# Second attention: turned probabilities applied as full fp32 on four 32-column tiles instead of as two fp32r parts on the whole array

## What is computed

```python
q = (x @ Wq).reshape(b, t, N_HEADS, HEAD_DIM).transpose(0, 2, 1, 3)
k, v = ...                       # N_KV = 8 heads, rotated q and k
k_h = jnp.repeat(k, GROUP_SIZE, axis=1)      # GROUP_SIZE = 4
v_h = jnp.repeat(v, GROUP_SIZE, axis=1)
scores = jnp.einsum('bhqd,bhkd->bhqk', q, k_h) / math.sqrt(HEAD_DIM)
scores = jnp.where(causal[None, None], jnp.finfo(scores.dtype).min, scores)
attn = jax.nn.softmax(scores, axis=-1)
ctx = jnp.einsum('bhqk,bhkd->bhqd', attn, v_h)
ctx = ctx.transpose(0, 2, 1, 3).reshape(b, t, D_OUT)
return ctx @ Wo
```

## Time and profile before

| | us |
|---|---|
| median of 3 runs | 1215.43 (1215.10 to 1216.92) |
| the profiled execution | 1214.89 |
| its span, first to last instruction | 1213.3 |
| in it: slots 4 to 62 of the loop, start to start | 198.24 |
| TensorE busy in these 198.24 | 196.56 |
| ScalarE busy in these | 197.38 |
| VectorE busy in these | 169.76 |
| GpSimd busy in these | 141.02 |

### The profile page before, as it was taken

How to read it: one execution, slowest core, us unless ns; L and a number is a source line. 1 busy time by engine, 2 the same in 40 slices (tenths; PEclk the granted TensorE clock), 3 DMA queues, 4 the chain that set the end, 5 groups by cost and what they waited for, 6 DMA issues and landing times. The chain is left out here.

```text
span 1213.3 us, 21135 instructions
## 1 busy us (share of the span) xinstructions
PE 1180.8 (97%) x6698; PEld 1023.2 (84%) x6698; DVE 799.6 (66%) x2575; ACT 752.5 (62%) x1758; POOL 548.3 (45%) x519
## 2 busy tenths in 40 slices
PE   7899999999999999999999999999999999999997
PEld 6788888888888888888888788888887999999886
DVE  6757776667766677766777722223458888888685
ACT  6656765566655567655665454441129999999624
POOL 4554454444533554534533233331136766676400
PEclk9999999999999999999999999999999999999999
DMA  6011110011110111101000022220002213220001
GB/s 223 18 44 36 35 36 28 22 43 27 46 34 12 44 36 35 36 27 35 27 1 27 18 70 78 61 97 1 18 20 53 65 41 108 48 48 21 1 1 70
DMA packets 30368, 51.28 MB, mean 42 GB/s; under 512 B 5680, under 2 KB 6576, under 8 KB 30256
## 3 DMA queue, kind: packets, MB, share of 16 engines
q1 hardware_dynamic: 29680, 48.85, 13.7%
q10 hardware_dynamic: 576, 1.05, 0.2%
HBM read 38.35 MB, written 2.10 MB: 33 GB/s over the span
## 5 line engine op out<-in xcount | busy, mean ns | idle before, releaser
L487 POOL TENSOR_TENSOR turned<-turned,sin 128x512 f32<-128x512 f32 x73 | 94.4, 1293 | 311.5 <-ACT turned L347 311.5
L363 ACT ACTIVATE probs<-probs,neg_max 128x256 f32<-128x256 f32 (+1 forms) x256 | 119.8, 473 | 14.0 <-DVE neg_max L580 14.0
L1484 ACT ACTIVATE a_probs<-a_probs,a_neg_max 128x512 f32<-128x512 f32 (+3 forms) x256 | 123.2, 571 | 0.1
L1720 DVE CUSTOM_DVE_ANT_0 a_probs<-bank,a_mask 128x512 f32<-128x512 f32 (+3 forms) x256 | 109.7, 485 | 0.2 <-PE bank L1949 0.2
L490 POOL TENSOR_TENSOR turned<-turned,by_cos 128x512 f32<-128x512 f32 x73 | 101.1, 1385 | 5.7
L96 PE MATMUL bank<-wo_hi,oT_hi 128*128 128x512 f32 x256 | 100.3, 392 | 1.7 <-DVE oT_lo L643 1.7
L734 PE MATMUL bank<-xT_hi,wq_hi 128*128 128x512 f32 x256 | 101.7, 397 | 0.0
L734 PE MATMUL bank<-xT_lo,wq_hi 128*128 128x512 f32 x256 | 100.2, 391 | 0.0
L734 PE MATMUL bank<-xT_hi,wq_lo 128*128 128x512 f32 x256 | 100.1, 391 | 0.0
L96 PE MATMUL bank<-wo_hi,oT_lo 128*128 128x512 f32 x256 | 99.9, 390 | 0.0
L96 PE MATMUL bank<-wo_lo,oT_hi 128*128 128x512 f32 x256 | 99.7, 389 | 0.0
(11 more groups left out here) (239 smaller groups left out, 3454.0 us busy)
## 6 DMA issues: line engine op xcount, KB each, us to landing
staged<-weights SPq DMA_DIRECT2D x70, 256.0 KB, 2.7
f_staged<-weights_f SPq DMA_DIRECT2D x33, 256.0 KB, 2.7
a_q_stack<-a_qT_hi SPq DMA_DIRECT2D x64, 64.0 KB, 2.0
rows<-x_rows SPq DMA_DIRECT2D x2, 1024.0 KB, 7.4
a_k_stack<-a_kT_hi SPq DMA_DIRECT2D x64, 32.0 KB, 2.0
a_q_stack<-a_qT_lo SPq DMA_DIRECT2D x32, 64.0 KB, 2.0
out<-rows SPq DMA_DIRECT2D x8, 256.0 KB, 2.0
a_raw<-weights_qkv SPq DMA_DIRECT2D x4, 384.0 KB, 4.9
```

What stands on the lines that cost most here:

```text
L363: act.activation(probs[:, s % 2, h, 0:width], probs[:, s % 2, h, 0:width], ACT.Exp, bias=neg_max[:, s % 2, h:h + 1], scale=SCALE0, accum_o ...
L487: pool.tensor_tensor(at, at, sin[:, :], ALU.mult).then_inc(sin_done, 1)
L1484: act.activation(row_probs(s, qt), row_probs(s, qt), ACT.Exp, bias=neg_max[:, h, qt:qt + 1], scale=-1.0).then_inc(exp_done, 1)
L1720: dve.tensor_tensor_reduce(row_probs(s, qt), ps_s[bank][:, at:at + seen], mask[:, SEQ - seen:SEQ], -SCALE1, HIGHEST, ALU.add, ALU.min, neg ...
```

## The change

A head's turned probabilities are no longer split. They are copied out of PSUM as plain fp32 into a ring of six heads, `pT`: piece 0 by VectorE, pieces 1 and 2 by ScalarE. GpSimd does nothing to them. The values stay plain fp32 too, in `v_tok`, 18 columns for a key tile (16 values, a one, and one more); a stationary operand is 32 columns of it, of which 17 count.

`apply` now works on a unit: for each key tile, four products, one for each head of the group, with the same 32 stationary columns, each to its own 32 partitions of one PSUM bank, on its own 32-column tile of the array (`tile_position`). The products are full fp32. Key tiles 0 and 3 come in the first slot after the unit, 1 and 2 in the second. Two banks take turns as `ps_o`. One result bank holds four heads instead of two, so `evacuate` (moved from ScalarE to VectorE), `turn_output` and `join` come once a unit instead of twice; `join` multiplies from PSUM straight to `o_tok`, and `finish` is gone.

The diff, cut to its core:

```diff
-HALF = P // 2
-ONE_AT = 2 * HD1
-PAIRS1 = 2 * UNITS1
+RING = 6
+VALUE_COLS = HD1 + 2
+HEAD_ROWS = P // GROUP1
+APPLY_KEYS = ((0, 3), (1, 2))
...
-            def high_turned(s):
-                if s >= 2:
-                    act.wait_ge(applied, s - 1)
-                act.wait_ge(pT_ready, PIECES * s + 1)
-                act.activation(pT_raw[:, s % 2, :], ps_t[0][:, :], ACT.Copy).then_inc(pT_copied, 1)
+            def copy_turned(s):
+                if s >= RING:
+                    act.wait_ge(applied, 2 * ((s - RING) // GROUP1 + 1))
                 for piece in (1, 2):
...
-                    act.activation(pT_hi[:, s % 2, piece, 0:width], ps_t[piece][:, 0:width], ACT.Copy).then_inc(pT_hi_done, 1)
-
-            def evacuate(n):
-                act.wait_ge(applied, 2 * (n + 1))
-                if n >= 1:
-                    act.wait_ge(o_turned, n)
-                act.activation(oT_now[:, :], ps_o[:, :], ACT.Copy).then_inc(o_read, 1)
+                    act.activation(pT[:, s % RING, at:at + width], ps_t[piece][:, 0:width], ACT.Copy).then_inc(pT_act, 1)
...
+            def copy_turned(s):
+                if s >= RING:
+                    dve.wait_ge(applied, 2 * ((s - RING) // GROUP1 + 1))
+                dve.wait_ge(pT_ready, PIECES * s + 1)
+                dve.tensor_copy(pT[:, s % RING, 0:SEQ], ps_t[0][:, :]).then_inc(pT_dve, 1)
+
+            def evacuate(n):
+                dve.wait_ge(applied, 2 * (n + 1))
+                if n >= 1:
+                    dve.wait_ge(o_turned, n)
+                dve.tensor_copy(oT_now[:, :], ps_o[n % 2][:, :]).then_inc(o_read, 1)
...
+                dve.reciprocal(inv_sum[:, :, :], turned[:, :, :, HD1]).then_inc(inv_done, 1)
                 dve.wait_ge(inv_done, n + 1)
-                dve.tensor_tensor(o_sum[:, :, :, :], turned[:, :, :, 0:HD1], o_sum[:, :, :, :], ALU.add).then_inc(summed, 1)
+                dve.tensor_tensor(o_tok[...].rearrange(
+                    "p t (h d) -> p t h d", d=HD1), turned[:, :, :, 0:HD1],
+                                  inv_sum[...].broadcast_to(
+                                      [P, SEQ_TILES, GROUP1, HD1]), ALU.mult).then_inc(finished, 1)
...
-            def apply(s):
+            def apply(u, part):
...
+                if u >= 2 and part == 0:
+                    pe.wait_ge(finished, u - 1)
+                if part == 0:
+                    pe.wait_ge(pT_dve, GROUP1 * (u + 1))
+                    pe.wait_ge(pT_act, 2 * GROUP1 * (u + 1))
+                for kb in APPLY_KEYS[part]:
                     piece, at = TURNED_AT[kb]
-                    width = SEQ - kb * P
-                    for part in (pT_hi, pT_lo):
-                        mm = pe.matmul(ps_o[:, kb * P:SEQ], v_now[:, u % 2, kb, window:window + P],
-                                       part[:, s % 2, piece, at:at + width],
-                                       start=(h % 2 == 0 and kb == 0 and part is pT_hi),
-                                       stop=(h % 2 == 1 and kb == KEY_TILES[-1] and part is pT_lo),
-                                       skip_group_check=True)
+                    at += piece * SEQ
+                    value = (u * SEQ_TILES + kb) * VALUE_COLS
+                    for h in range(GROUP1):
+                        mm = pe.matmul(ps_o[u % 2][h * HEAD_ROWS:(h + 1) * HEAD_ROWS, kb * P:SEQ],
+                                       v_flat[:, value:value + HEAD_ROWS],
+                                       pT[:, (GROUP1 * u + h) % RING, at:at + SEQ - kb * P],
+                                       start=(kb == APPLY_KEYS[0][0]), stop=(kb == APPLY_KEYS[-1][-1]),
+                                       skip_group_check=True, tile_position=(0, h * HEAD_ROWS))
                 mm.then_inc(applied, 1)
...
-            for s in range(SLOTS1 + 1):
+            for s in range(SLOTS1 + 2):
                 if s < SLOTS1:
                     turn(s)
-                if BEHIND_APPLY <= s < SLOTS1 + BEHIND_APPLY:
-                    apply(s - BEHIND_APPLY)
+                if s >= GROUP1 and s % GROUP1 < 2:
+                    apply(s // GROUP1 - 1, s % GROUP1)
...
-                if s % 2 == 1 and s >= 3:
-                    turn_output((s - 3) // 2)
+                if s % GROUP1 == 3 and s >= GROUP1:
+                    turn_output(s // GROUP1 - 1)
```

More of the change, by code:

```diff
@@ L1282, in attention1 @@
         k_tok = sb("k_tok", [P, TILES, KV1 * HD1])
-        v_tok = sb("v_tok", [P, UNITS1, SEQ_TILES, HD1])
+        v_flat = sb("v_tok", [P, UNITS1 * SEQ_TILES * VALUE_COLS + HEAD_ROWS])
+        v_tok = v_flat[:, 0:UNITS1 * SEQ_TILES * VALUE_COLS].rearrange("p (u t c) -> p u t c", u=UNITS1, t=SEQ_TILES)
         o_tok = q_tok
         probs = sb("probs", [P, GROUP1, HEAD_PROBS])
[L1289 to L1293, removed]
+        pT = over("pT", [P, RING, HEAD_PROBS], xT_at)
+        b_at = aligned(nc.sbuf_base)
+        sb("b_place", [P, 2, D])
         oT_now = sb("oT_now", [P, SEQ])
-        o_sum = sb("o_sum", [P, SEQ_TILES, 2, HD1])
         by_at = aligned(nc.sbuf_base)
@@ L1451, in _ @@
                     sp.dma_start(small[:, :], small_in).then_inc(main_in, 16)
-                    for n in range(2):
-                        sp.dma_start(main_raw[n][:, :, :], w_f1[2 * n:2 * n + 2].rearrange("k p c -> p k c")[:, :, 0:D]).then_inc(main_in, 16)
+                    for place, some in ((main_first, slice(0, 1)), (main_rest, slice(1, KC))):
+                        sp.dma_start(place[:, :, :], w_f1[some].rearrange("k p c -> p k c")[:, :, 0:D]).then_inc(main_in, 16)
             for tile in range(TILES):
@@ L1505, in _ @@
                     norm.high(act, TILES - 2 + tile)
+                if tile == 0:
+                    act.wait_ge(pads_set, 2)
                 copy_values(tile)
@@ L1657, in side_weight @@
                                    ALU.subtract).then_inc(side_lo_done, 1)
[L1659 to L1664 removed]
+            turn_rows(TILES - 1)
+            for s in range(2, SLOTS1):
+                pool.wait_ge(pT_dve, s)
                 if s in OUT_SLOTS:
                     out_weight(OUT_SLOTS.index(s))
[L1667 to L1670 removed]
                 if SIDE_SLOT <= s < SIDE_SLOT + KC:
@@ L1750, in _ @@
             rotate(TILES - 1)
-            for s in range(SLOTS1 + 2):
+            for s in range(SLOTS1 + 3):
+                if s % GROUP1 == 2 and s >= GROUP1:
+                    evacuate(s // GROUP1 - 1)
                 if s + AHEAD_MAXIMA < SLOTS1:
@@ L2023, in turn_out @@
             def turn_out(tile):
[L2024 removed]
+                pe.wait_ge(finished, UNITS1 * (tile // SEQ_TILES + 1) // BATCH)
                 if tile >= 2:
```

142 lines of the change are left out of this document (39 added, 103 removed).

## The result

| | before | after |
|---|---|---|
| median of 4 runs each, us | 1215.38 | 1179.26 (1178.34 to 1180.21) |
| ratio, 95% interval | | 0.970 (0.968 to 0.972) |
| the profiled execution, its span | 1214.89, 1213.3 | 1180.05, 1178.4 |
| first four slots | 16.05 | 16.11 |
| slots 4 to 62, start to start | 198.24 | 163.26 |

What follows compares the result with a forecast made beforehand. TensorE and ScalarE were both taken as full in the second attention's loop; a unit of 8.36 + 2a, with a = 1.5, falls from 13.44 to 11.36 us, -31 us, to 1184 us. Own range 1168 to 1201; wider range to 1228.

Steps and rivals of the forecast that it cites:

- VectorE 10.3, copy 0.6: VectorE in the second attention's loop: 10.3 us a unit, a floor, with a new 512-column PSUM copy at 0.6 us.
- The evacuation's wait: VectorE, head of every fourth slot: evacuation waits for apply's second part; costed at nothing, up to 0.3 us a unit.
- The price of a column, 1.75 ns: TensorE: a full fp32 product is two matmuls of 0.88 ns a column each, four fp32r passes.
- The part, `a`: TensorE, one of a unit's two apply blocks, four heads side by side: 1.5 us, ends 1.1 and 2.05.
- The upper bound by weight loads: TensorE, apply: 32-column loads take as long as 128-column ones; 16 loads of 0.11 make 1.74, plus 0.3 us.
- The slots: Second attention's loop: two slots with apply take 1.78 us plus 1.5 each; two light ones, ScalarE late, 4.8 together.
- The sum: Four-slot unit of the loop: 11.36 us, 2.08 less than 13.44, over 14.75 units: -31 us.
- The clock: TensorE in the loop: a granted clock falling under 1.00 would mark the forecast as wrong.
- Around the loop: First four slots left at 16.05 us (at most -4); the end 4.85 against 4.94, no change; transfers keep their bytes.
- Rival 1: TensorE, apply: program-order starts let only neighbouring heads overlap; 2.7 us per apply block, 1222 us; chance 0.33.
- Rival 2: TensorE, apply: four heads' products follow each other, not side by side; 4.8 us per block, 1288 us; chance 0.15.
- Rival 3: VectorE and ScalarE copies and evacuation bind earlier through mutual waits; unit 12.2 to 12.8 us, 1201 us; chance 0.07.

Runs made afterwards that it cites:

- one pass: Changed kernel with turned probabilities and values kept as bf16 for apply, so each product is one matmul of one pass; 1165.45 us, ratio 0.959.
- the run with the heads outside: Changed kernel with apply's two loops exchanged, each head's key tiles standing ahead of the next head's; 1179.88 us, ratio 0.971.
- the best version: Changed kernel with apply's second part two slots after the first, ahead of the transposes, and the evacuation on VectorE in slot 2; 1174.79 us, ratio 0.967.

## Why the prediction was right

The forecast, 1184 us, was 4.7 us too high; the measured 1179.26 lies in its own range and on its side. Its core holds: four heads run side by side, at the price a column that it took, and ScalarE's relief was needed. What it said of the short slots is right in the number by luck, as told below. Point by point:

- **What bounds the kernel.** Two engines at once, as read from the earlier trace rows. The runs with work put back on ScalarE show both halves: with ScalarE loaded the two short slots grow, with TensorE loaded (one tile) the two long ones do, 6.38 and 6.35 us.
- **ScalarE 10.2 us a unit.** Right: 2.55 us a slot from start to start and 10.15 a unit where it is never idle (one pass).
- **VectorE 10.3, copy 0.6.** The copy is right: 0.60 from start to start (1004.29 less 1003.69, the evacuation, of the same size). The sum was slightly high: 10.19 from start to start in the run with one pass, mostly since the product of 256 columns takes 0.34 and not 0.42. As a floor it was so 0.1 too high; that loop ran at 10.15 on average, its last two slots being short.
- **The evacuation's wait.** Costed at nothing, up to 0.3 us a unit. It is there, 4.2 us in 14 waits, 0.30 each, and it reaches TensorE, which waits for VectorE's copy behind it. The run without the evacuation on VectorE won 0.10 us a unit, and that run took the 0.6 us of work off VectorE too.
- **The price of a column, 1.75 ns.** Right: 1.73.
- **The part, `a`.** Forecast 1.5, made up of 1.12 for streaming, 0.3 for entry and exit and 0.08 for starts that don't coincide. From the first product to the scores it is 1.21, but that leaves out the entry, which falls ahead of the first product. From the first start to the last it is 0.905, and the last matmul streams for 0.215: 1.12, of which 0.02 (and not 0.08) are starts that don't coincide and 0.02 more are what a part's first matmul takes beyond the next of its size (0.347 and 0.323). Entry and exit were mis-sized: the last transpose and the first product start 0.20 us apart, where transposes follow each other in 0.11, and the last product and the scores 0.31, where such a matmul streams in 0.215. That is 0.09 + 0.10 = 0.19 us a part, under the 0.3 taken and far under the 0.5 of the bound, and the whole is 1.30 to 1.31 us. The Trainium skill ("TensorEngine Tiling (Array Packing)", Key Properties) says that a change of mode drains TensorE. There is a gap at both ends, of 0.1 us each, but a full drain isn't seen in the records: the first product starts 0.07 us before the last transpose ends (1002.336, and 1002.134 + 0.273), and the scores start 0.07 us before the last product ends (1003.551, and 1003.241 + 0.379). These ends are modelled, so the rows don't settle it.
- **The upper bound by weight loads.** Not reached: sixteen loads of 106 to 110 ns are in a part of 1.21 us, where one behind the other they'd take 1.74. They overlap across tiles; four start within 20 ns like their matmuls.
- **The slots.** Long ones 3.17 and 3.14, forecast 3.28 (1.78 + 1.5), so 0.25 less for two; the scores took 0.745 and not 0.68, which took back some of the part's saving. Short ones 4.71, forecast 4.8. The number is near, the reason was another: the forecast has ScalarE late at 2.55 us a slot, less up to 0.4 that it is ahead. In the trace ScalarE is nowhere in the chain that ended last. VectorE's late copy ends the third slot (2.47), and the fourth (2.24) is TensorE's own work, for which the forecast had 1.8 to 2.1.
- **The sum.** A unit is 11.03 and not 11.36. The loop was forecast at 198.24 - 30.7 = 167.5 us and took 163.26, 4.3 less, about the whole difference between 1184.2 and the profiled 1180.05. Two things in it weren't forecast and cancel by chance: slot 4 at the lower clock, 1.6 us more, and the last two slots of the loop, in which no scores are left to make, 2.40 and 1.60 us and not 3.14 and 2.47, 1.6 us less.
- **The clock.** The prediction counts a granted clock under 1.00 in the loop as a sign of being wrong. It was 0.99, by the one stretch in slot 4, for 1.6 us of the 35.0 won; the rest of the loop has 1.00, so the account of the other slots stands.
- **Around the loop.** First slots unchanged, right; the tail 4.47 and not 4.85, since two parts take 2.29 us there (1095.60 to 1097.89) and not 3.0:

```profile
1093.42 1.28 PE L1899 MATMUL bank<-identity,a_probs 128*128 128x128 f32 x10 [0.29 <-DVE f_pT L1669]
1094.54 0.60 PE L1932 MATMUL bank<-identity,a_oT_now 128*128 128x128 f32 x4
1095.60 2.36 PE L1920 MATMUL bank<-f_pT,a_v_tok 128*32 128x512 f32 x32 [0.46 <-ACT f_pT L1486]
1097.89 1.09 PE L1978 MATMUL bank<-identity,a_q_tok 128*128 128x128 f32 x8
```

- **Rival 1** is refuted by the starts, and by the run with the heads outside. The Trainium skill ("TensorE: Matmul & The Clock Gate", Part 3) says both that tiles run concurrently and that starts follow the order of the program; of the two the first holds here, with four starts within 20 ns, and the second doesn't across tiles, with eight starts of 384 columns ahead of the first of 256. **Rival 2** is refuted by the starts as well; what it would have cost is the run on one tile, 1281 us, 1288 worked out. **Rival 3** didn't come: a unit is 11.03 us and not over 12; the handing over costs little, the waits listed above.

What stays open: why the clock fell in the loop in some profiles (the changed kernel's two and one more) and not in others with the same work ahead of it; and the half microsecond between the 5.1 us that the best version's loop wins without that slot and the 4.6 of the medians.

## What to carry to other kernels

When two engines are full for the whole of a loop, a change wins only what it takes from both; count what it takes from each, and put the work it creates on the one that has room (here VectorE, 170 of 198 us busy but 0.93 us a slot of it leaving). Small products with 32 or fewer stationary columns can go side by side on column tiles: full fp32 at four passes then costs about what a single fp32r pass of each head in turn would (1.21 us a part, against 2,560 columns at 0.44 ns, 1.13 us, an estimate from the earlier trace rows), and saves the splitting, its copies and its low parts on three engines. Where such a block of work is put matters too: behind the scores and not ahead of them it let the other engines start earlier, and that, with the evacuation moved to fit, was worth another 4.6 us.

## What the hardware showed

- Column tiles take their matmuls independently. Four heads' matmuls start within 20 ns (7 ns from one to the next), and within 40 ns (13 ns from one to the next) where the program puts four matmuls of one head ahead of the next head's first.
- Each matmul of a full fp32 product streams at 0.84 to 0.85 ns a column on 32-column tiles: 0.429 us from start to start for 512 columns, 0.109 for 128. The first one of a part takes 0.024 us more (0.453 for 512), on four tiles as on one.
- Weight loads of 32 columns last 106 to 110 ns each, and those of four tiles overlap.
- Going from the whole array to tiles and back cost 0.09 us each way beyond the usual pitch: starts are 0.202 us apart on entry, where transposes are 0.109 apart; at the exit 0.309 behind a matmul of 256 columns (0.215) and 0.202 behind one of 128 (0.109). The run on one tile has the same 0.202 and 0.309, so it isn't the number of tiles.
